# Layer 0 of a graph network on one Trainium2 core: one bank for the low sums, two for the edge counts, and another order of work per slot

## The reference, cut to what matters

```python
agg  = segment_sum(x[src], dst, num_segments=12500)
mean = agg * inv_deg[:, None]
h    = x @ W_self + mean @ W_neigh + b       # relu after layers 0 and 1
...
x = x + ffn(layernorm(x))                    # top half of the tokens by a routing weight
```

## Time and profile before

| what | us |
|---|---|
| median of 3 runs (6059.19 to 6067.04) | 6063.86 |
| profiled execution, its own time | 6064.39 |
| its span | 6062.2 |
| GpSimd busy in it | 3912.0 |
| TensorE busy in it | 4166.2 |
| VectorE busy in it | 2811.4 |

### The profile page before, as it was taken

One profiled execution on the slowest core, in us unless ns is written; L12 is line 12 of the kernel. 1 busy time (PEld: TensorE's weight loads), 2 busy tenths in 40 slices (PEclk: granted clock), 3 DMA queues, 4 the chain that ended last, 5 costly groups with the idle time before them and its releaser, 6 DMA issues.

```text
span 6062.2 us, 112776 instructions
## 1 busy us (share of the span) xinstructions
PE 4166.2 (69%) x20492; PEld 2675.0 (44%) x20878; DVE 2811.4 (46%) x8126; ACT 1056.5 (17%) x2551; POOL 3912.0 (65%) x4094
## 2 busy tenths in 40 slices
PE   0444566666666667845778766666569999889992
PEld 0122233333333335523556433333257887667772
DVE  7223455555554445512222333344234445666666
ACT  7000011111111112200000100111012223334440
POOL 0777566665544447667777777776777765777760
PEclk9867788888888889976889988888689999999996
DMA  7555455555544446656777666666567775666655
GB/s 243 156 156 145 125 161 165 166 153 152 149 127 133 135 135 182 177 153 186 230 235 246 205 180 181 185 186 171 158 205 221 232 225 154 175 174 176 170 152 173
DMA packets 565085, 1065.85 MB, mean 176 GB/s; under 512 B 154587, under 2 KB 361983, under 8 KB 558527
## 3 DMA queue, kind: packets, MB, share of 16 engines
q0 software_dynamic: 261376, 803.21, 46.2%
q10 hardware_dynamic: 196564, 228.51, 11.0%
q1 hardware_dynamic: 106987, 32.54, 2.3%
HBM read 928.09 MB, written 135.83 MB: 175 GB/s over the span
## 4 chain that ended last, share of the span: by engine, by line
PE 24%; issue 23%; POOL 22%; DMA 9%; DVEq 9%; DVE 9%; ACT 2%; ACTq 1%; POOLq 0%; SPq 0%
POOL gath L619 22%; DMA gath<-table,idx_ring 7%; PE agg L826 6%; PE y L903 4%; PE hid L893 3%; DVE onehot L1155 3%; PE agg L828 3%; DVEq L1155 2%; DVEq L1214 2%; PE lo L765 2%; PE y L678 1%; DMA idx_ring<-idx_dram 1%; DVEq L1258 1%; PE count_ps L765 1%; ACTq L1502 1%
## 5 line engine op out<-in xcount | busy, mean ns | idle before, releaser
L619 POOL DMA_INDIRECT gath<-table,idx_ring x4084 | 3910.5, 958 | 1986.6 <-issue 1380.9
L826 PE MATMUL agg<-gath,onehot 128*128 x4831 | 1980.4, 439 | 985.0 <-SPq L546 799.6
L1155 DVE TENSOR_SCALAR onehot<-iota_row,window_base,dst_f 128x128 f32 x3584 | 1013.8, 360 | 1276.4 <-PE agg L828 478.3
L826 PEld LDWEIGHTS agg<-gath,onehot 128*128 x5216 | 560.4, 107 | 2122.0 <-issue 1788.3
L828 PE MATMUL agg<-gath,onehot 128*128 x3264 | 969.0, 297 | 184.6 <-SPq L546 139.9
L1148 DVE TENSOR_TENSOR onehot<-count_ps,dst_f 128x512 f32 x408 | 282.3, 692 | 827.7 <-PE agg L828 714.7
L903 PE MATMUL y<-w_sb,hidT 128*128 128x256 f32 x1568 | 368.6, 389 | 26.4 <-ACT hidT L1666 25.8
L828 PE MATMUL hid<-gath,onehot 128*128 x924 | 297.8, 322 | 122.4 <-SPq L546 105.6
L828 PEld LDWEIGHTS agg<-gath,onehot 128*128 x3264 | 338.6, 104 | 83.5
L828 PE MATMUL lo<-gath,onehot 128*128 x1028 | 342.0, 333 | 44.4 <-issue 18.9
L893 PE MATMUL hid<-featT,w_gnn 128*128 128x128 f32 x3136 | 366.9, 275 | 0.0
(11 more groups left out here) (182 smaller groups left out, 3962.1 us busy)
## 6 DMA issues: line engine op xcount, KB each, us to landing
gath<-table,idx_ring POOLq DMA_INDIRECT x4084
dense<-counts_dram ACTq DMA_DIRECT2D x50, 1024.0 KB, 6.4
table<-split ACTq DMA_DIRECT2D x194, 192.0 KB
counts_dram<-dense ACTq DMA_DIRECT2D x16, 1600.0 KB, 9.0
rows_f<-y ACTq DMA_DIRECT2D x194, 128.0 KB
dense<-rows_f ACTq DMA_DIRECT2D x48, 512.0 KB, 9.4
table<-gath ACTq DMA_DIRECT2D x24, 768.0 KB, 3.6
xb<-x ACTq DMA_DIRECT2D x97, 128.0 KB
```

The source lines that it names most:

```text
L619: g.indirect_dma_start(gath[:, j, 0:PARTS * D], None, table[layer][:, :], bass.IndirectOffsetOnAxis(ap=idx_ring[:, h, i:i + 1], axis=0)).t ...
L826: mm(agg[p][:, 0:2 * D], oh, tile_rows[:, :, 0:2 * D], start=False, **flags)
L1155: last = v.tensor_scalar(onehot[:, bass.ds(pair, GROUP), :][:, j, :], iota_row[:], window_base[:, col(w)], dst_f[:, bass.ds(tiles, GROUP)] ...
```

## The change

It does the following, all in layer 0.

- The low sums have one bank for both parities. ScalarE copies it with the degree column to `lo_sb[p]` (`copy_low`, first in its slot), VectorE's `mean_done` reads the copy, and TensorE waits for `lo_copied` before it clears the bank for the next window.
- The bank that this frees takes every second group of the counts; TensorE may begin a group when the copy before the last is done, no longer the last.
- `layer_product` in layer 0 waits for `self_ready` (L1118) instead of `lo_ready` (L1121).
- The bounds of a slot's two groups are packed into one word, loaded with one register load (two in the first slot of a turn) and taken apart with shifts and masks. Two small instructions make the words, once.
- The counting loop is cut in two. The first four turns (slots 6 to 21) keep the interleaving. In the other twelve (slots 22 to 69) a slot's order is: TensorE counts the whole first group, aggregates the window in one span, counts the second group. VectorE: one-hots of the first group, of the window in one span, `mean_done`, `split_product`, one-hots of the second group. ScalarE has a new order too, with the copy of the product early and the count copies after the split's second part.
- The one-hots of a block stay four instructions.

```diff
+COUNT_PIECED = 4
+    COUNT_SPLIT = COUNT_AT + COUNT_PIECED * 4
+    COUNT_LOOPS = [(COUNT_AT, COUNT_SPLIT, 4), (COUNT_SPLIT, COUNT_END, 4), (COUNT_END, LAST_LOOPED, 2)]
...
-        agg_lo = [lo0[:], hid[:, 0, :]]
+        agg_lo = lo0[:]
+        count_banks = [count_ps[:], hid[:, 0, :]]
...
+        def group_bounds(eng):
+            ends = []
+            def end_of(value):
+                return eng.snap(value, min_val=0, max_val=TILES - 1)
+            def both_groups(turn, j):
+                def packed(k):
+                    return eng.value_load(group_pairs[0:1, col(turn * 4 + k)], min_val=0,
+                                          max_val=2 ** (2 * TILE_BITS) - 1)
+                if j == 0:
+                    ends[:] = [end_of(packed(0) >> TILE_BITS)]
+                here = packed(j + 1)
+                first, mid, end = ends[0], end_of(here & (2 ** TILE_BITS - 1)), end_of(here >> TILE_BITS)
+                ends[:] = [end]
+                return (first, mid), (mid, end)
+            return both_groups
...
                 if phase == 1 and (not isinstance(n, int) or n):
-                    pe.wait_ge(lo_ready, n)
+                    pe.wait_ge(self_ready, n)
...
                 def first_half():
-                    pe.wait_ge(count_copied, g + 2)
-                    mm(count_ps[:, 0:1], zeros[:], ones_bf[:, 0:1], start=True, stop=False, skip_group_check=True)
+                    pe.wait_ge(count_copied, g + 1)
+                    mm(bank[:, 0:1], zeros[:], ones_bf[:, 0:1], start=True, stop=False, skip_group_check=True)
...
                 if layer == 0:
-                    mm(agg_lo[p][:, 0:1], zeros[:], ones_bf[:, 0:1], start=True, **free)
+                    if not isinstance(n, int) or n:
+                        pe.wait_ge(lo_copied, n)
+                    mm(agg_lo[:, 0:1], zeros[:], ones_bf[:, 0:1], start=True, **free)
...
+                if steps and part[0] == 0:
+                    steps[0]()
+                    aggregate(0, w, half, p, part, steps[1:])
+                elif steps:
+                    steps[0]()
+                    steps[1]()
+                    aggregate(0, w, half, p, part)
+                    steps[2]()
+                    steps[3]()
...
             def mean_done(n, p):
-                dve.wait_ge(agg_ready, n + 1)
-                v.tensor_scalar(deg[0:r, :], agg_lo[p][0:r, D:D + 1], 1.0, None, ALU.max).then_inc(deg_ready, 1)
+                dve.wait_ge(lo_copied, n + 1)
+                v.tensor_scalar(deg[0:r, :], lo_sb[p][0:r, D:D + 1], 1.0, None, ALU.max).then_inc(deg_ready, 1)
...
-                v.tensor_scalar(mean, agg_lo[p][0:r, 0:D], inv, None, ALU.mult).then_inc(lo_added, 1)
+                v.tensor_scalar(mean, lo_sb[p][0:r, 0:D], inv, None, ALU.mult).then_inc(lo_added, 1)
...
+                if steps:
+                    steps[0]()
+                if steps and part[0] == 0:
+                    onehots(0, w, half, p, part, steps[1:])
+                else:
+                    if steps:
+                        steps[1]()
+                    if exists(w):
+                        onehots(0, w, half, p, part)
                 if exists(w - 1):
                     mean_done(w - 1, 1 - p)
                 if exists(w - 4):
                     split_product(1, w - 4, p, part)
+                if steps and part[0] == 1:
+                    steps[2]()
+                    steps[3]()
...
+            def copy_low(n, p):
+                r = rows(n)
+                act.wait_ge(agg_ready, n + 1)
+                if not isinstance(n, int) or n >= 2:
+                    act.wait_ge(mean_ready, n - 1)
+                a.copy(lo_sb[p][0:r, :], agg_lo[0:r, 0:D + 1]).then_inc(lo_copied, 1)
...
+                if exists(w - 1):
+                    copy_low(w - 1, 1 - p)
+                if counting and part[0] == 1:
+                    copy_product(1, w - 4, earlier(half, p, 4), p)
+                    copy_rows(w - 1, 1 - p)
+                    relu0(w - 3, 1 - p)
+                    copy_zT(w - 2, p)
+                    copy_rest(1, w - 4, p, part)
+                    if j == 0:
+                        act.wait_ge(counts_stored, turn * 16 + 16)
+                    copy_counts(j * 2)(turn * 8 + j * 2)
+                    store_parts(1, w - 4, p, part)
+                    copy_counts(j * 2 + 1)(turn * 8 + (j * 2 + 1))
+                    if j == 3:
+                        store_counts(turn)
+                    return
```

More of the change, by code:

```diff
@@ L301, in gnn_ffn_program @@
         lo_added = sem("lo_added")
+        lo_copied = sem("lo_copied")
         mid_added = sem("mid_added")
@@ L860, in slot_layer0 @@
                     count_ends()
[L861 to L867, removed]
+                steps = []
+                if part and part[0] < 2:
+                    turn = part[1] + (0, COUNT_PIECED)[part[0]]
+                    bounds = pe_groups(turn, part[2])
+                    steps = [step for j in range(2) for step in count_group(
+                        turn * 8 + (part[2] * 2 + j), bounds[j], count_banks[j])]
+                if steps and part[0] == 0:
[7 more added lines that the diff above has]
+                    steps[3]()
+                elif exists(w):
+                    aggregate(0, w, half, p, part)
             over_windows(pe, 4, COUNT_LOOPS, slot_layer0)
@@ L1255, in tile_onehots @@
                     slot = dve.snap((t + g) % COUNT_RING)
+                    tile = nc.s_assert_within(
+                        dve.snap(t), 0, TILES - 1,
+                        skip_runtime_bounds_check_because="tiles are counted from the sorted edges, below TILES")
                     dve.wait_ge(count_used, t + 2)
@@ L1278, in slot_layer0 @@
                     split_sources()
[L1279 to L1285, removed]
+                steps = []
+                if part and part[0] < 2:
+                    turn = part[1] + (0, COUNT_PIECED)[part[0]]
+                    bounds = dve_groups(turn, part[2])
+                    steps = [step for j in range(2) for step in count_onehots(turn * 8 + (part[2] * 2 + j), bounds[j])]
+                if steps:
[7 more added lines that the diff above has]
+                        onehots(0, w, half, p, part)
                 if exists(w - 1):
@@ L1499, in split_store, with copy_rest @@
                 a.copy(split[p][0:r, 0, :], y).then_inc(hi_ready, 1)
+            def copy_rest(phase, n, p, part):
+                r, w = rows(n), window_of(phase - 1, n, part)
                 act.wait_ge(rest_ready, upto(phase, n))
@@ L1507, in split_store @@
                               split[p][0:r, :, :].rearrange("p t d -> p (t d)")).then_inc(stored[p], 16)
+            def split_store(phase, n, half, p, part):
+                copy_product(phase, n, half, p)
+                copy_rest(phase, n, p, part)
+                store_parts(phase, n, p, part)
             def copy_counts(j):
@@ new lines, in copy_zT, with relu0 @@
+            def copy_zT(n, p):
+                r = rows(n)
+                act.wait_ge(z_tp_ready, n + 1)
+                if not isinstance(n, int) or n >= 2:
+                    act.wait_ge(hT_ready, n - 1)
+                a.copy(zT[p][:, :, 0:r], tp[:].rearrange("p h (k n) -> p (h k) n", n=P)[:, :, 0:r]
+                       ).then_inc(zT_ready, 1)
+            def relu0(n, p):
+                r = rows(n)
+                act.wait_ge(hT_ready, n + 1)
+                if not isinstance(n, int) or n >= 2:
+                    act.wait_ge(mm_ready, upto(1, n - 2))
+                for m in range(KD):
+                    last = a.activation(featT[p][:, m, 0:r], hT[:, m, 0:r], ACT.Relu, bias=bias0[:, m:m + 1])
+                last.then_inc(featT_ready, 1)
@@ L1602, in slot_layer0 @@
             def slot_layer0(w, half, p, part):
+                counting = part and part[0] < 2
+                if counting:
+                    turn, j = part[1] + (0, COUNT_PIECED)[part[0]], part[2]
                 if exists(w - 1):
-                    n, r = w - 1, rows(w - 1)
-                    if not isinstance(n, int) or n >= 2:
-                        act.wait_ge(z_tp_ready, n - 1)
-                    a.copy(xb[1 - p][0:r, :], resid[0:r, col(n), :].rearrange("p n d -> p (n d)")
-                           ).then_inc(ln_copied, 1)
@@ L1626, in slot_layer0 @@
-                if part and part[0] == 0:
-                    turn, j = part[1], part[2]
+                    copy_low(w - 1, 1 - p)
[13 more added lines that the diff above has]
+                    return
```

69 lines of the change are left out of this document (36 added, 33 removed).

## The result

| | us |
|---|---|
| before, median of 4 (6059.19 to 6067.04) | 6061.81 |
| after, median of 4 (5914.74 to 5917.75) | 5915.31 |
| ratio, with its 95% interval | 0.9758 (0.9741 to 0.9775) |
| forecast | 5886, range 5800 to 5980 |
| profiled execution of after, its own time | 5917.75 |

The account below looks back on a forecast made before the run. VectorE with its register work was taken to bound slots 22 to 69. Terms of 191 us less 35 for queueing gave 156, plus 20 and 2 elsewhere made 178, so 6064 became 5886 us, range 5800 to 5980.

Parts of the forecast that it names:

- Bounds: Slots 22 to 69, VectorE: fewer register loads before the first count one-hot save 1.9 us a slot, 91 us.
- One span instead of four: Slots 22 to 69, VectorE: three fewer openings and ways back to the counts save 1.4 us a slot, 67 us.
- ScalarE's order at the turn: Twelve turn slots: issuing the counts' store last removes 1.6 us of extra waiting each, 19 us; lower bound 0.
- Second bank and `self_ready`: Slots 22 to 69: freeing TensorE is worth only VectorE's waits for it, 14 us, between 0 and 28.
- Low sums through ScalarE: Layer 0: one more copy a slot on a little-used ScalarE costs nothing, hidden behind other work.
- The turn stays at 5.90 us: Loop's turn, VectorE: the gap behind the branch remains 5.90 us, as the body still has four slots; no gain counted.
- rival 1: The stall at the loop's turn goes too, as one-hot code copies leave the body: 5815 us; chance 0.10.
- The queue between near-equal stages: Slots 22 to 69: gathers, TensorE and VectorE come near in pace, so 35 us (0 to 110) is lost.
- rival 2: TensorE or the ring becomes the bound; coupling costs 2 to 3 us a slot, 5982 us; chance 0.14.
- a sign of being wrong: Slots 22 to 69: VectorE waiting for `lo_copied` or ring slots by more than 1 us a slot would refute the forecast.
- Rival 3: Slots 22 to 69: TensorE falls to its lower clock, 1.2 GHz, making the kernel slower, 6264 us; chance 0.05.
- Rival 4: No gain: waits only change place, with `mean_done` waiting for ScalarE; 6042 us or above; chance 0.05.

Follow-up runs that it names:

- Bounds alone: The kernel before with only the packed bounds added: 7371.83 us, 0.9869 of the kernel before, with pauses.
- four loads: The changed kernel with the four register loads of bounds put back in each slot: 1.0122, 1.0113 and 1.0137 of the kernel before, all with pauses.
- old order: The changed kernel with all 16 turns interleaved as before: 5943.23 us, 0.9820 of the kernel before without pauses; 0.9889 and 0.9872 with pauses.
- group 1: A set of follow-up runs with sequencer pauses, each compared with the kernel before on the same chip; ratios there 0.9869 to 1.0122.
- group 3: The one set of follow-up runs without sequencer pauses, each compared with the kernel before on the same chip; ratios there 0.9724 and 0.9820.

## Why the prediction was right, and where its sum was off

The forecast's direction, cause and range held. All terms below are of slots 22 to 69, where idle times are summed over the instructions of the stretch.

**Bounds, 91 us: right.** With all of the change but the new order the stretch is 90.1 us shorter. The idle time at the head of the 48 slots, where the loads stand, fell from 267 to 175 us, which is 92. Bounds alone (-96) and four loads (+87), over all 64 slots, agree, both with pauses. At the head of an ordinary slot 1.6 us were forecast, and the changed kernel has 1.5 to 1.7 on the mean.

**One span instead of four, 67 us: the term that failed.** An ordinary slot takes 20.44 us before, 18.44 in the old order and 18.34 in the new one; the forecast was 17.8. The new order itself gave 0.1 us a slot where 1.4 stood. I had priced openings and ways back as if each stood alone. Two rows show what I missed:

```profile
1612.00 0.29 DVE L1304 TENSOR_SCALAR dense<-iota_row,dense 128x128 f32 x1
...
1615.62 1.12 DVE L1193 TENSOR_SCALAR onehot<-iota_row,window_base,dst_f 128x128 f32 x4 [0.30 <-issue]
```

These are of the old order. Back from a span to the counts VectorE had nearly no idle time (no bracket at 1612.00; median of 85 such places 0.14 us), since the sequencer works ahead while the one-hots run. And blocks that follow one another in the single span wait 0.30 us or more at 145 places where 60 were, many of them 0.50 as in the timeline above. All idle time in front of and behind window one-hots fell only from 158.6 to 135.7 us, -23 where 67 stood, and the second group pays a new opening of 0.65 us behind the split in each of the 48 slots, 31 us, which my count of openings left out. The 135.7 us hold 36.4 us of waiting for ring slots where the 158.6 held 15.5, so that 21 us more of what was saved went into the coupling of the stages.

**ScalarE's order at the turn, 19 us: right.** The wait for the split's middle part fell from 50.2 to 32.0 us, 18, all of it in the turn slots (2.2 to 0.7 us).

**Second bank and `self_ready`, 14 us (0 to 28): at its lower bound.** Bounds alone and the old order differ by nothing that can be told with pauses; without them the heads of the slots account for 92 of the 90.1 us of the old order, and leave nothing for the banks. The wait of `layer_product` for the split is gone, as forecast.

**Low sums through ScalarE, 0: no cost was seen.** No wait of VectorE for `lo_copied` stands among those of the stretch; it is part of the same two comparisons.

**The turn stays at 5.90 us: half wrong, and not for rival 1's reason.** The gap behind the branch is still there in all turns of both loops, but in slots 22 to 69 it is 3.6 us on the mean of 11 turns, where the old order has 5.8 on 12. With the loads that grew to 0.93 us beside it, the head of the slot at the turn fell from 8.4 to 7.5 us only. The instruction packets fell by 13, about one a turn. As far as the traces show, what shortened the gap is where the store of the counts stands. Those with pauses move the store about under one and the same body of four slots. In the first run of the old order it is issued 14.7 us before the branch that ends at 1447.88, and the gap is 3.31 us; it is issued 5.8 us before the branch that ends at 2034.15, and the gap is 6.20 (each time the store and the first count behind the turn):

```profile
1433.14 0.39 ACTq L1589 DMA_DIRECT2D counts_dram<-dense  x1
...
1453.85 0.28 DVE L1304 TENSOR_SCALAR dense<-iota_row,dense 128x128 f32 x1 [5.70 <-issue]
```

```profile
2028.38 0.39 ACTq L1589 DMA_DIRECT2D counts_dram<-dense  x1
...
2043.01 0.29 DVE L1304 TENSOR_SCALAR dense<-iota_row,dense 128x128 f32 x1 [8.59 <-issue]
```

All turns in the old order, in every trace with four slots in the body, go the same way. Where the store was issued 8 us or more before the branch, the gap is 2.8 to 4.1 us (17 turns); where it was issued 4.5 to 8 us before, it is 5.7 on the mean (73 turns, 3.0 to 6.7). In slots 22 to 69 of the changed kernel the store comes 1.6 to 2.6 us behind the branch. Nor does the smaller body by itself give a short gap: in the second run with four loads it has 4.9 to 6.0 us at the four turns where the store came 1.4 to 2.8 us before the branch, and 1.3 to 2.9 at the other seven. (Where the store comes less than 1.5 us before the branch, both kinds occur.) Whether the size takes a smaller part is open, and a kernel that moves the store alone was not run. By the Trainium skill ("Runtime: NRT & Kernel Launch", section on instruction fetch mechanics) a taken branch to a target outside the window of two pages waits for a fetch. The runs agree on VectorE: with a body of two slots the gap is gone and 122 packets became 30.

**The queue between near-equal stages, -35 us: rightly there.** VectorE's wait for ring slots went from 9.6 us before to 15.5 in the old order and 36.4 in the new, TensorE's for gathered rows from 13.9 to 57.7. That is rival 2's mechanism at a fraction of its price: GpSimd still waits 230.8 us for TensorE, forecast 200, and VectorE's 36.4 us are 0.8 a slot, under the 1 us that I had named as a sign of being wrong. Waits of engines that run side by side can't be added up, so whether the term was 35 us is not shown.

Together: forecast 191 - 35 = 156; measured 90 for the loads and 33 for the new order, 123. The 33 stand almost wholly at the turn: the twelve turn slots went from 27.2 to 24.8 us on the mean (forecast 23.7), 29 us, the other 36 slots gave 4. In the turn slots the wait for the split's middle part fell by 18 us and VectorE's idle time before counts by 25, while that before window one-hots rose by 13. In the other 36 all its idle time before counts and one-hots went from 218 to 215 us. So the single span gave nothing that can be seen, and 67 was the miss. It was hidden in part because the turn, which I had set at nothing, gave something; that the forecast is only some 30 us off owes something to luck. Slots 6 to 21 gave 24.7 (forecast 20), the rest of layer 0 lost 3 (forecast a gain of 2).

**The rivals.** Rival 1, the stall gone, did not come with this body. A body of two slots removes the stall, but with the old order 56 us of the 88 come back (5887.55 us), and with the new order and pauses none that can be told. Rival 3 fell: the granted clock rose. Rival 4 fell: the loads' gain is there in full. With pauses the new order costs 92 us. In slots 22 to 69 VectorE waits there 28.3 us for ring slots instead of 11.9, GpSimd 628.8 instead of 543.3, which is like rival 2; that this is the cause is argued, not shown.

## What to carry to other kernels

Register loads in the head of a loop's slot are path, not overhead: packing four into one or two gave some 90 us of the 146.5 in slots 22 to 69 alone, and the waits show them only as "issue". Price an opening or a branch by the idle time in front of the next busy instruction, not by its own length, for a sequencer that works ahead hides a part of it, and count the openings that the new order adds. Where a branch shows a gap of several microseconds behind it, try a body half as long before any new order: here that was worth 56 us without pauses, where the new order was worth 28. And look at which transfer is under way when the branch is taken: here a large store just issued goes with a gap that is some 2 us longer.

## What was not expected of the hardware

**Pauses.** In three of four groups the sequencers of some engines stop for some 0.7 us, many times. The rows of the same line in the changed kernel's two runs (first the one without pauses; shortest, median and longest in ns):

```profile
L1193 DVEq FUSED_REGOPS  x4480: 53/93/254, 146.6 to 5760.8; - x195
```

```profile
L1193 DVEq FUSED_REGOPS  x4480: 1/93/1397, 146.5 to 7197.9; - x195
L1203 DVEq ALU_OP  x1639: 3/45/1379, 146.1 to 7195.4; - x183
```

The median is the same and the longest is 1,397 ns, twice 0.7. In that run 1,152 register instructions of VectorE, 1,328 of TensorE and 271 of SyncE take over 0.4 us, 6 of ScalarE and none of GpSimd; in the undisturbed runs of before, after and the old order there are none. VectorE's register work as a whole grows from 1532 to 2172 us and the kernel by 1,440. The pauses come in groups, often at the same moments on several engines, and here they go with a run of gathers of GpSimd without a break, from 1908.61 us, which themselves keep their 0.95 us:

```profile
1908.61 0.99 POOL L646 DMA_INDIRECT gath<-table,idx_ring  x1 [11.25 <-PE lo L857]
1909.90 0.95 POOL L646 DMA_INDIRECT gath<-table,idx_ring  x1 [0.30 <-issue]
...
1927.58 0.95 POOL L646 DMA_INDIRECT gath<-table,idx_ring  x1 [0.30 <-issue]
```

The pauses that belong to this run last from 1917.9 to 1931.2 us: they set in 9 us behind the first gather and end some 3 us behind the last. What makes them is not settled. They are no lasting property of a chip: group 1, with them, and group 3, without, ran on the same one, half an hour apart. Their effect on a result is large: the same change measures 0.9758 without and 1.0002 with them.

**The price of a load depends on what else moves.** The register load of 0.31 us takes 0.93 us at the loop's turn of the changed kernel, 1 to 4 us after the 1,600 KB store was issued, and up to 1.6 us. Of VectorE's 24 loads that began before such a store had landed, 23 took 0.71 to 1.60 us; at the turns of the kernel before, where the store lands before the loads begin, they take 0.30 to 0.33:

```profile
L455 DVEq TENSOR_LOAD <-group_pairs x80: 300/319/1604, 651.3 to 2105.9; - x80
```
